# A two-part block over eight images, software-pipelined by hand: key-value products in 64x64 blocks, one transpose for all coefficients, the second norm's variance on ScalarE, and a new written-out order

## What is computed

```
x = x + attention(norm_over_channels(x))
  q, k, v = 1x1 convolutions;  Q = elu(q) + 1, K = elu(k) + 1
  out[l] = Q[l] (sum over m <= l of K[m]^T v[m]) / (Q[l] . sum over m <= l of K[m])
t = tokens(x)
t = t + sum over the two chosen experts e of
        prob_e * (gamma_e * (norm(t) @ expert_w[e] + expert_b[e]) + beta_e)
  prob = softmax(norm(t) @ gate_w + router_gamma), top 2 kept
```

## Time and profile before

| | |
|---|---|
| time, median of 3 runs | 754.56 us (754.48 to 757.04) |
| the profiled execution: time, span | 755.91 us, 754.1 us |
| busy, share of the span: PE, DVE, ACT, POOL | 95%, 91%, 54%, 53% |
| PE in the chain that ended last | 91% |
| mean granted TensorE clock | 0.982 of full |

### The profile page before, as it was taken

The page is one execution under the profiler, slowest core; times in us unless marked ns, Lnnn a source line. Parts: engine busy times, 40 slices in busy tenths (PEclk is TensorE's granted clock), DMA queues, the critical chain, the costliest instruction groups (busy, mean ns, idle before and its releaser), DMA issues.

```text
span 754.1 us, 23195 instructions
## 1 busy us (share of the span) xinstructions
PE 717.1 (95%) x8137; PEld 624.0 (83%) x8137; DVE 685.9 (91%) x2550; ACT 409.9 (54%) x1261; POOL 397.8 (53%) x639
## 2 busy tenths in 40 slices
PE   4767999999999999999999999999999999999986
PEld 2666888888888888888888888888888888888875
DVE  4567999999999999999999999999999999999984
ACT  1122666655555666666665555555555555555544
POOL 5145555555555555555555555555555555555520
PEclk9769999999999999999999999999999999999999
DMA  5101111111111111111111111111111111111101
GB/s 129 33 15 30 42 40 35 37 40 37 39 37 42 42 42 42 42 42 42 42 42 42 42 42 42 42 42 42 42 42 42 42 42 42 42 30 29 30 16 29
DMA packets 60214, 30.29 MB, mean 40 GB/s; under 512 B 2160, under 2 KB 60176, under 8 KB 60176
## 3 DMA queue, kind: packets, MB, share of 16 engines
q1 hardware_dynamic: 60176, 29.79, 14.4%
HBM read 20.34 MB, written 9.44 MB: 39 GB/s over the span
## 4 chain that ended last, share of the span: by engine, by line
PE 91%; DVE 4%; POOL 2%; ACT 1%; issue 1%; DMA 1%; SPq 0%; DVEq 0%; ACTq 0%; POOLq 0%
PE bank L877 11%; PE bank L915 10%; PE bank L894 9%; PE bank L916 9%; PE bank L917 9%; PE bank L933 8%; PE bank L901 4%; PE bank L909 4%; PE bank L884 4%; PE bank L853 3%; PE bank L854 3%; PE bank L855 3%; PE bank L860 3%; PE bank L847 2%; PE bank L866 2%; PE bank L935 2%
## 5 line engine op out<-in xcount | busy, mean ns | idle before, releaser
L574 DVE TENSOR_TENSOR probs<-bank,tri 128x512 f32<-128x512 f32 x288 | 184.9, 684 | 10.2 <-PE bank L877 4.7
L397 ACT ACTIVATE y_act<-bank,scale 128x128 f32<-128x128 f32 x576 | 159.4, 383 | 2.5
L915 PE MATMUL bank<-e_high,x_high 128*128 128x512 f32 x288 | 124.0, 431 | 1.1 <-DVE o L803 1.1
L916 PE MATMUL bank<-e_low,x_high 128*128 128x512 f32 x288 | 113.7, 395 | 0.0
L917 PE MATMUL bank<-e_high,x_low 128*128 128x512 f32 x288 | 113.5, 394 | 0.0
L311 POOL TENSOR_TENSOR qn<-feat,rden 128x512 f32<-128x512 f32 x36 | 38.2, 1061 | 116.4 <-DVE rden L672 116.4
L416 ACT ACTIVATE x_high<-x 128x512 fp32r<-128x512 f32 x36 | 22.8, 633 | 137.0 <-DVE x L664 137.0
L592 DVE SCALAR_TENSOR_TENSOR y_dve<-bank,scale,y_dve 128x128 f32<-128x128 f32 x288 | 92.4, 343 | 0.0
L580 DVE SCALAR_TENSOR_TENSOR qkv<-bank,rstd,b_qkv 128x384 f32<-128x384 f32 x144 | 86.8, 605 | 5.1 <-POOL rstd L301 2.6
L387 ACT ACTIVATE k_odd<-bank,parity 128x512 f32<-128x512 f32 x36 | 24.7, 687 | 114.4 <-PE bank L860 114.4
L933 PE MATMUL bank<-ident,y_act 128*128 128x128 f32 x576 | 80.8, 273 | 1.6 <-ACT y_act L397 1.6
(11 more groups left out here) (139 smaller groups left out, 1764.5 us busy)
## 6 DMA issues: line engine op xcount, KB each, us to landing
x<-in_x SPq DMA_DIRECT2D x36, 256.0 KB, 3.3
x_res<-in_x SPq DMA_DIRECT2D x36, 256.0 KB, 3.2
out<-o SPq DMA_DIRECT2D x36, 256.0 KB, 2.4
beta_raw<-in_L_ffn_beta_w SPq DMA_DIRECT2D x1, 512.0 KB
e_raw<-in_L_ffn_expert_w SPq DMA_DIRECT2D x1, 512.0 KB
w_raw<-in_L_conv_Wkv SPq DMA_DIRECT2D x2, 64.0 KB, 2.4
b_qkv<-in_L_conv_bkv SPq DMA_DIRECT2D x1, 128.0 KB, 4.4
w_raw<-in_L_conv_Wq SPq DMA_DIRECT2D x1, 64.0 KB, 2.6
```

The source lines that it names most:

```text
L397: last = nc.scalar.activation(y_act[:, p, u, e], bank[EXPERTS_AT[u][0]][:, 128 * e:128 * e + 128], ACT.Copy, scale=scale[:, p, u, e:e + 1])
L574: return tt(probs[:, half, i].rearrange("p u e t -> p (u e) t"), bank[SCORES_AT[half][i]][:].rearrange("p (n t) -> p n t", t=T), tri[:].un ...
L915: mm(out, x1_high[:, p, u], e_high[:, w], start=True, stop=False)
L916: mm(out, x1_high[:, p, u], e_low[:, w], start=False, stop=False)
```

## The change

It has four parts, and PoolE's instructions stay the same ones.

1. `key_values`: for each unit two 64x64 products (the two halves of the heads) take the place of one 128x128 product of which the mask threw most away. The mask on DVE becomes two instructions on 64 partitions with 4x64 elements each (`masked_blocks`). The rest of `kv_new` is zeroed once.
2. Coefficients: `coef3` is packed so that all four units' coefficients stand in 128 columns. `turn_coef` is one transpose where it was four, ACT's copy `coef_t` is 128x128 where it was 96x512, and `bias` is four 128-column products, each with weights of its own (`bias_rows`, built once from transposes), where it was one of 512 columns.
3. Second norm: `turn_x1` multiplies by the centring matrix, so the turned x1 has its mean taken off. DVE's four bn_stats and the bn_aggr group fall away. ACT takes the variance by four Square activations with an accumulated sum (`variance`).
4. New order: LAGS is 7, so 42 steps. Feature instructions move to `g[3]`, most attention work to `g[4]` and `g[5]`, the experts to `g[6]`. The two halves of `values` stand apart, the exponential of the logits opens ACT's step, and the bank numbers are new.

```diff
-LAGS = 6
+LAGS = 7
-AT = dict(x=4, kv=3, att=6, x1_a=6, x1_b=4, k=1, q=7, coef=0, out=1)
-SCORES_AT = ((3, 7, 2, 0), (0, 5, 6, 7))
+AT = dict(x=6, kv=3, att=7, x1_a=7, x1_b=6, k=4, q=5, coef=2, out=3)
+SCORES_AT = ((0, 1, 2, 7), (0, 2, 5, 3))
...
-                make(copy(id_gate[:, 0:T], ident[:]))
+                make(copy(id_gate[:, 0:T], centre[:]))
...
+                dve.wait_ge(S["rest_pe"], 4)
+                turned = bank[WEIGHTS_AT[3]][:, 0:EXPERTS]
+                make(copy(bias_high[:], turned))
+                dve.wait_ge(S["rest_dve"], done[0])
+                for u in range(U):
+                    make(copy(bias_cols[:, u, u, 0:2], bias_high[:].bitcast(F32).unsqueeze(1).broadcast_to([128, 2, EXPERTS])))
+                    make(tt(bias_cols[:, u, u, 2], turned, bias_high[:].bitcast(F32), ALU.subtract))
+                assert done[0] == REST_COLS
+                dve.wait_ge(S["rest_pe"], 5)
+                make(copy(bias_rows[:].rearrange("p u d -> p (u d)"), bank[WEIGHTS_AT[0]][:]))
                 assert done[0] == REST_PSUM
...
+            def variance(p, units):
+                for u in units:
+                    last = nc.scalar.activation(squares[:, u], x1_units[u], ACT.Square, scale=CH ** -0.5,
+                                                accum_out=mv2[:, p, u, 1:2])
+                return last
...
+            def masked_blocks():
+                new = bank[AT["kv"]][:, 0:64 * U].rearrange("p (u d) -> p u d", u=U)
+                for i in range(2):
+                    rows = slice(64 * i, 64 * i + 64)
+                    last = tt(kv_new[rows, :, rows], new[rows],
+                              pair_mask[rows].unsqueeze(1).broadcast_to([64, U, 64]), ALU.mult)
+                return last
...
             def key_values(p):
                 for u in range(U):
-                    last = mm(bank[AT["kv"]][:, 128 * u:128 * u + 128], feat[:, p, u, 128:256], qkv[:, p, u, 256:384],
-                              start=True, stop=True)
+                    for i in range(2):
+                        last = mm(bank[AT["kv"]][64 * i:64 * i + 64, 64 * u:64 * u + 64],
+                                  feat[:, p, u, 128 + 64 * i:128 + 64 * i + 64],
+                                  qkv[:, p, u, 256 + 64 * i:256 + 64 * i + 64], start=True, stop=True)
...
             def turn_coef(p):
-                for u in range(U):
-                    last = transpose(bank[AT["coef"]][0:3 * QUAD, T * u:T * u + T], coef3[:, p, u].bitcast(F32), ident[:])
+                return transpose(bank[AT["coef"]][:, 0:T], coef3[:, p].rearrange("p u s e -> p (u s e)").bitcast(F32), ident[:])
             def bias(p):
-                return mm(bank[AT["out"]][:], e_bias3[:], coef_t[:, p], start=True, stop=False, skip_group_check=True)
+                for u in range(U):
+                    last = mm(bank[AT["out"]][:, T * u:T * u + T], bias_rows[:, u], coef_t[:, p], start=(u == 0),
+                              stop=False, skip_group_check=True)
...
+                if g[5]:
+                    n, p = g[5].i, g[5].par
+                    need(pe, "probs_00", n + 1)
+                    need(pe, "probs_02", n + 1)
+                    need(pe, "out", n - 1)
...
+                    scores(p, 1).then_inc(S["scores_1"], 1)
```

More of the change, by code:

```diff
@@ new lines, in step @@
+                if g[3]:
+                    p = g[3].par
+                    pad_values(p, 0).then_inc(S["v_pad_0"], 1)
+                if g[5]:
+                    n = g[5].i
+                    need(act, "x1_var_b", n + 1)
+                    nc.scalar.activation(lg_raw[:, IN_N], bank[AT["x1_b"]][:, T:WIDE], ACT.Copy)\
+                        .then_inc(S["lg_raw_b"], 1)
+                if g[6]:
+                    n, p = g[6].i, g[6].par
+                    need(act, "experts_11", n + 1)
+                    weigh_one(p, 1).then_inc(S["y_one_1"], 1)
@@ new lines, in step @@
+                if g[4]:
+                    n, p = g[4].i, g[4].par
+                    need(act, "q_turned", n + 1)
+                    nc.scalar.activation(q_t[:, p].rearrange("p u t -> p (u t)"), bank[AT["q"]][:], ACT.Copy)\
+                        .then_inc(S["q_t"], 1)
+                if g[6]:
+                    n, p = g[6].i, g[6].par
+                    need(act, "coef_turned", n + 1)
+                    need(act, "bias", n - 1)
+                    nc.scalar.activation(coef_t[:, p], bank[AT["coef"]][:, 0:T], ACT.Copy).then_inc(S["coef_t"], 1)
+                    need(act, "experts_01", n + 1)
+                    weigh_one(p, 0).then_inc(S["y_one_0"], 1)
@@ new lines, in step @@
+                if g[5]:
+                    n, p = g[5].i, g[5].par
+                    need(dve, "values_1", n + 1)
+                    need(dve, "values_0", n + 1)
+                    dve.wait_ge(x_res_loaded[p], 16 * (g[5].half + 1))
+                    tt(flat(x1, p), bank[AT["att"]][:], flat(x_res, p), ALU.add).then_inc(S["x1"], 1)
+                if g[3]:
+                    n, p = g[3].i, g[3].par
+                    need(dve, "exps_0", n + 1)
+                    features(p, 0).then_inc(S["feat_0"], 1)
@@ L654, in step @@
                 if g[5]:
                     n = g[5].i
[L656 to L664 removed]
+                    need(dve, "lg0", n + 1)
@@ L879, in scores @@
                 return last
-            def from_state(p):
-                for u in range(U):
-                    last = mm(bank[AT["att"]][:, T * u:T * u + T], state[:, U * p + u], q_t[:, p, u],
-                              start=(u == 0), stop=False, skip_group_check=True)
-                return last
             def values(p, half):
@@ new lines, in step @@
+                if g[6]:
+                    n, p = g[6].i, g[6].par
+                    need(pe, "kv_new", n + 3)
+                    if k is not None:
+                        need(pe, "probs_13", n + 2)
+                        need(pe, "out", n)
+                    experts(p, 1, 1).then_inc(S["experts_11"], 1)
+                    need(pe, "coef_low", n + 1)
+                    need(pe, "y_dve_32", n + 1)
+                    if k is not None:
+                        need(pe, "probs_11", n + 2)
+                    turn_coef(p).then_inc(S["coef_turned"], 1)
@@ new lines, in step @@
+                    scores(p, 0).then_inc(S["scores_0"], 1)
+                if g[6]:
+                    n, p = g[6].i, g[6].par
+                    need(pe, "coef_t", n + 1)
+                    need(pe, "y_dve_12", n + 1)
+                    if k is not None:
+                        need(pe, "kv_new", n + 3)
+                    bias(p).then_inc(S["bias"], 1)
+                if g[0]:
+                    n, p = g[0].i, g[0].par
+                    pe.wait_ge(x_loaded[p], 16 * (g[0].half + 1))
+                    need(pe, "y_dve_02", n - 5)
+                    if k is not None:
+                        need(pe, "x1_var_b", n - 4)
+                        need(pe, "lg_raw_b", n - 4)
+                        need(pe, "x_parts", n)
+                    turn_x(p).then_inc(S["x_turned"], 1)
@@ L954, in step @@
+                if g[4]:
+                    n, p = g[4].i, g[4].par
+                    need(pe, "probs_03", n + 1)
+                    if k is not None:
+                        need(pe, "qkv_0", n + 3)
+                    from_state(p).then_inc(S["from_state"], 1)
                 if g[3]:
```

870 lines of the change are left out of this document (416 added, 454 removed), and 13 rows, old and new, of the table names.

## The result

The changed kernel takes 777.9 us (median of 4 runs, 776.4 to 779.5) against 755.4 for the kernel before: a ratio of 1.030, 95% interval 1.028 to 1.032. The forecast was 740 and faster. The profiled execution took 776.4 us with a span of 774.4.

The account below looks back on a forecast made before the run. PE was taken as the bound, DVE 4% behind; its step was to fall to 18.73 us, 18.78 with 0.05 allowed for waits. 95 + 29 x 18.78 + 100.1 = 739.7, so 740 us, range 730 to 757.

Parts of the forecast that it names:

- DVE's slack: DVE in the loop: its 18.5 us busy a step become 17.5, 1.2 under the step.
- The start: Before the full steps: a seventh stage and a longer weight stage, so step 7 starts at 95 us.
- the end: Steps 36 to 41, where projections are missing and the steps get shorter: 100.1 us.
- terms of PE: PE's step, block by block: changes sum to -0.48 us, so 18.73 a step if PE never waits.
- Key-values: Key-value products on PE as 16 overlapping 64x64 records: 0.54 us for 0.90, so -0.36 a step.
- rival A: Key-value products on PE: the 64x64 blocks take turns on one bank; 0.41 in 34 steps, 754 us; chance 0.13.
- rival B: Bias products on PE go at float32's pace: 0.81 us, 0.37 x 34 more, 752.6 us; chance 0.12.
- changes of kind: PE blocks behind another kind or array shape: fewer longer first float32r products, one more shape change, together -0.05 us.
- The tight places: PE's scores waiting for `out` fit by 0.09 us, `turn_x1` waiting for x1 by 0.01; 0.05 a step allowed for both.
- Rival C: ACT's squares make PE's experts wait, each costing s more: 4s - 0.5 a step, kernel slower, up to 762 us; chance 0.09.
- DVE's masks: Key-value masking on DVE as two instructions of half the elements: 0.75 us for 0.69.
- D: Blocks and everything fit better than counted, bias at 0.33 and ends 5 us shorter: 730 us; chance 0.05.

Follow-up runs that it names:

- the first experiment: The changed kernel with three waits added on POOL: x1_low until DVE's rank_a is done, qk until hot_a, state until lg2; 749.1 us, ratio 0.991.

## Why the prediction was wrong

**The step that failed** is the sentence on DVE's slack, "Its 18.5 busy (184.92 / 192 of a step) become 17.5, 1.2 under the step.", with "POOL's same work keeps 7 us of slack" behind it. DVE's own work was right to the digit: 176.26 / 192 x 19.05 = 17.5 us in the first experiment. But I took each engine's durations as its own. POOL's work is the same; its places against DVE's changed, and with 2.56 us of standing still a step DVE was busy for 19.7 (189.70 / 192 x 19.98), all but 0.2 of the step. Slack of an engine tells whether it can be late, not whether it is in another's way. No rival priced this, although three rows at the end of before showed it (one stands above), and a 128x32 row of 1.18 us, where its like take 0.18, should have been followed up. Every place that I laid out was a wait on a semaphore.

In the account of the span: the prediction had 95 + 29 x 18.78 + 100.1 = 739.7; measured 92.3 + 29 x 19.98 + 102.5 = 774.4. The start was 2.7 better, the end 2.4 worse, and the loop has the whole miss, 34.8 us. Of these, 29 x (19.98 - 19.05) = 27 are the three pairs, and 29 x (19.05 - 18.78) = 8 are terms of PE. With the pairs out of the way the time is in the stated range and of the right sign, 749.1 against 740, but the gain is 7 us where some 15 were forecast.

**The terms of PE** are mis-sized, their mechanism right. From PE in order of time of the first experiment, to be read beside the earlier trace rows:

```profile
403.49 0.69 PE L941 MATMUL bank<-qkv,feat 128*64 128x64 f32 x16
404.11 0.44 PE L899 MATMUL bank<-w_high,x_high 128*128 128x384 f32 x1
...
407.58 0.27 PE L970 MATMUL bank<-ident,coef 128*128 128x128 f32 x1
407.74 0.63 PE L912 MATMUL bank<-ident,qn 128*128 128x128 f32 x4
...
412.02 0.66 PE L975 MATMUL bank<-coef_t,bias_rows 128*128 128x128 f32 x4
412.52 0.62 PE L893 MATMUL bank<-ident,x 128*128 128x128 f32 x4
...
415.17 1.06 PE L949 MATMUL bank<-q_t,state 128*128 128x128 f32 x8
416.06 0.60 PE L906 MATMUL bank<-ident,feat 128*128 128x128 f32 x4
416.59 0.50 PE L923 MATMUL bank<-q_t,k_even 32*128 32x128 f32 x8
```

Key-values 0.62 for 0.54: the blocks overlap, since by the prediction's estimate 16 records one behind the other would be 0.85, so rival A is out. By the Trainium skill, "TensorEngine Tiling (Array Packing)", Restrictions and Gotchas, they would have taken turns; the measurement decides against that here. Coefficients 0.16 for 0.11, bias 0.50 for 0.44 (rival B, 0.81, is out), `from_state` 0.89 for 0.81 and `turn_k` 0.53 for 0.42, both with a new neighbour; 0.09 of the last only moved there, since the last y record costs 0.11 now (396.01 to 396.12) and cost 0.20 before. That is 0.29 a step of the 0.32 by which the 19.05 exceed the prediction's 18.73. I had booked the changes of kind as a gain of 0.05; they are a loss.

**The tight places** held. In the first experiment PE waits at neither, and the margins are wider than the 0.09 and 0.01 of the forecast, because the blocks that cover them are longer. In the step from 396.01, `out` ends at 397.16, with the 0.15 of the prediction 397.31, and the scores start at 397.54: 0.23. `x1` ends at 404.41, so 404.56, and `turn_x1` starts at 404.74: 0.18. **Rival C** did not come: the squares follow each other at 0.25 to 0.27 us, the second instruction that stores the sum (0.20) overlapping the next square, so s is 0 against the 0.29 of a weighting. **DVE's masks** of the key-values cost 0.88 for 0.75, without effect. **D** did not come either.

## What to carry to other kernels

Where an order is rewritten, lay DVE's small SBUF instructions beside POOL's long ones, in time, as a place of its own, whatever slack both have: a 0.18 us instruction can cost 1 us there, and three of them cost 29 us of 778. In a trace, look for a short form whose mean is several times that of its like, and for a neighbour on POOL that ends with it. The remedy is cheap: one wait that puts POOL's instruction behind DVE's last small one, or the POOL instruction in halves, and the kernel is 0.8 to 0.9% faster than before instead of 3.0% slower. Most of that gain doesn't need the new order: the two parts on PE alone, in the order of before, gave 0.6% (0.994, 0.992 to 0.996, against 0.991, 0.989 to 0.994, which is hardly apart).

## What the runs showed of the hardware

- Held beside a POOL `tensor_tensor` of two SBUF inputs until it ended: DVE's `tensor_tensor` and `scalar_tensor_tensor` with two SBUF inputs (to 1.20 us) and a float32 `tensor_scalar` from SBUF to SBUF (1.15). Not held: reductions, and instructions with an input in PSUM.
- A POOL `tensor_scalar` with one SBUF input, 1.49 us long, held a DVE `tensor_tensor` until 0.65 us behind its own start, 0.18 or 0.27 us in all. A POOL `memset` of 0.52 us held it not at all.
- Eight float32 products of 64x64 (16 records) took 0.62 us, two row halves writing one bank, for 0.90 as four of 128x128 (8 records). In the order of before they made the blocks on either side 0.10 and 0.07 us longer.
- An activation that accumulates has a second instruction of 0.20 us, and costs 0.25 to 0.27 from start to start all the same.
